# Softmax of the even heads: one ACTIVATE per head with an accumulated row sum, in place of subtract, one wide exponential and a reduction

## The chip, the cores and the metric

One core of a Trainium2 chip runs the whole program in one launch. The metric is device time in microseconds; the median of 3 runs is used. About 0.2% (9.5 us) is what a measurement of this kernel can tell from no change.

## The reference, cut to what matters

The input is `x` of shape (4, 512, 128). Four residual blocks follow each other: a gated linear attention, a transformer stack, a Mamba block, and the same transformer stack again. The change touches only the attention of the transformer stack, which runs twice with 6 layers each:

```python
def attn_layer(x, Wqkv, qs, ksc, Wo):        # HEADS 16, DIM_HEAD 64, WINDOW 32
    q, k, v = split(x @ Wqkv)                # per head
    q = l2norm(q) * qs; k = l2norm(k) * ksc
    q, k = rotary(q), rotary(k)
    # local attention: each window of 32 queries sees the 32 keys before it and its own 32
    sim = einsum('bhwie,bhwje->bhwij', bq, bk2) * QK_SCALE     # QK_SCALE 8
    sim = where(mask, -max, sim)
    attn = softmax(sim, -1)                  # over 64 keys
    out = einsum('bhwij,bhwje->bhwie', attn, bv2)
    return out @ Wo
for i in range(6):
    x = attn_layer(shift_tokens(x), ...) + x
    x = ffn_layer(shift_tokens(x), ...) + x  # layer norm, W1, a * gelu(gate), W2
```

So for every query and head there is a softmax over 64 scores: a maximum, an exponential of 8 * (score - max), and a sum by which the output is divided.

## The kernel before, in words

Each engine has its own hand-written instruction stream, tied to the others by counting semaphores; an engine works strictly in the order of its stream. The transformer stack is called a phase here: 24 bodies (6 layers x 4 batch rows), twice, so 48 bodies. A body handles one batch row of one layer and consists of 4 units (u = 0 to 3), one tile of 128 tokens each: 192 units in all. Most bodies run inside a hardware loop (`Fori`) on every engine, so there is a jump back once per body.

The work is software-pipelined. In unit u of a body, `pe_body`, `act_body`, `dve_body` and the loop in `pool_ffn` work on several tiles at once:
- the projection of tile u+2 in chunks of 512 columns (`pe_proj`, three matmuls per chunk, L273 to L275, chunk 0 one unit earlier than the rest). Chunks 0 to 3 are queries and keys: ScalarE squares each (`act_square`, L512), VectorE multiplies each by the rotary tables (`dve_rotate`, L693 to L695) and sums the squares (L696). VectorE waits at L691 for the square of the same chunk. Chunks 4 and 5 are values, copied out by ScalarE (`act_v`, L520);
- the norms of tile u+2 (`dve_rnorm` L716 to L723 on VectorE, `pool_newton` on GpSimd), and the rotated rows on GpSimd (L907, L913);
- the transposes of queries and keys of tile u+1 (`pe_qk_t`, L301), copied out by ScalarE (`act_qk_t`, L541), its scores (`pe_scores`, L329, L336) and its softmax (`dve_softmax_in`, `act_exp_odd`, `act_exp_even`);
- the transposed probabilities (`pe_probs_t`, L317, copied by `act_probs_t`, L548), the product with the values (`pe_pv`, L350) and the division (`dve_den`, `dve_out`, L760) of tile u;
- the output transposes of tile u-1 (L287, L530), and pieces of the projection Wo (L373) and of the MLP of the body before (L407, L408, L416; `act_gelu` L590, `act_std` L578, `dve_wo` L767, `dve_hidden` L796, `dve_down` L803).

The 16 heads are 8 pairs. Even heads (par 0, g = 0) have their scores in PSUM bank `s_ps[0]`, odd heads (g = 1) in `s_ps[1]`; each bank is 128 rows x 8 heads x 64 scores.

The softmax before: for the odd heads VectorE takes the maximum (L734) and scales it by -8 (L738, `bias_done`); ScalarE does 8 exponentials, one per head, each with that head's bias and an accumulated row sum (L558; the trace shows each as an ACTIVATE and an ACTIVATION_READ_ACCUMULATOR). For the even heads VectorE takes the maximum (L734) and subtracts it from the scores of all 8 heads in one instruction (L743, `sub_done`), ScalarE does one exponential over all 512 columns (L565, `exp0_done`), and VectorE reduces it to the row sums at the start of the next unit (L749 in `dve_den`), before the reciprocal (L753).

The order of ScalarE's stream around the change, from the end of one unit to the next:

```python
act_probs_t(it, u)            # L548
act_v(it, u + 2, 0); act_v(it, u + 2, 1)
act_exp_odd(it, u + 1)        # 8 x L558
act_square(it, u + 3, 0)      # L512
act_exp_even(it, u + 1)       # L565
# next unit (u is one higher now)
act_qk_t(it, u + 1, (0, 1))   # L541 q_t
act_square(it, u + 2, 1)      # L512
act_qk_t(it, u + 1, (2, 3))   # L541 k_t
```

VectorE's order in a unit is: rotate chunks 0 and 1, `dve_den`, `dve_xs`, rotate chunks 2 and 3, `dve_rnorm`, the pieces of the MLP, `dve_softmax_in`, `dve_out`. The queue of SyncE issues 16 DMAs per unit that copy the values into window pairs (`sp_pairs`, L943); `act_v` of the next tile waits for their landing.

## Time and profile before

| what | value |
|---|---|
| median of 3 runs | 4733.21 us (4729.46 to 4737.49) |
| span of the profiled execution | 4761.0 us |
| VectorE (DVE) busy | 3952.0 us, 83% |
| TensorE (PE) busy | 3888.7 us, 82% |
| ScalarE (ACT) busy | 2715.4 us, 57% |
| GpSimd (POOL) busy | 2320.0 us, 49% |
| mean granted TensorE clock | 0.906 |

For the profiled execution the span from its first to its last instruction is the only time that is given; it is 27.8 us (0.6%) above the median of the unprofiled runs. Busy shares are averages over the whole span; the transformer phases lie at about 120 to 2200 us and 2760 to 4640 us.

### The profile page before, as it was taken

To read this page: it belongs to the slowest core of one execution; us is meant where nothing else is said; L and a number is where in the kernel's file an instruction comes from. 1 tells how busy PE (TensorE), PEld (TensorE's weight loads), DVE (VectorE), ACT (ScalarE), POOL (GpSimd) and SP (SyncE) were. 2 spreads that over 40 slices of the span, in tenths; PEclk is the share of its full clock that TensorE was granted. 3 is DMA by queue.
4 is the path that set the end of the run, shared out by engine and by line. 5 is a ranking of instruction groups with operands and counts; after the bars stand their busy time and mean duration, and the time that the engine had idled before them with its cause. 6 is when DMAs were issued, how large, how long until landed. Compare 5 with 4: busy or idle time off the path is not lost. (4 is left out here: it accounts for less than half of the span.)

```text
span 4761.0 us, 167496 instructions
## 1 busy us (share of the span) xinstructions
PE 3888.7 (82%) x62204; PEld 2492.3 (52%) x62204; DVE 3952.0 (83%) x8550; ACT 2715.4 (57%) x6877; POOL 2320.0 (49%) x2468
## 2 busy tenths in 40 slices
PE   7788888888888888885655788888888888888887
PEld 2555565555555555552111365655655555555554
DVE  7798888888888888875888798888888888888884
ACT  2466566666656666662333366565656666566664
POOL 3455555555545555541444555455545545555551
PEclk9899999999989899996677789999998998998998
DMA  1222222222222222220000122222222222222221
GB/s 33 62 75 74 69 73 69 73 68 76 74 66 76 67 71 71 72 71 15 0 0 0 30 67 67 73 73 70 73 72 70 66 76 71 71 73 67 74 68 50
DMA packets 249055, 293.99 MB, mean 62 GB/s; under 512 B 61326, under 2 KB 136198, under 8 KB 248326
## 3 DMA queue, kind: packets, MB, share of 16 engines
q1 hardware_dynamic: 248446, 284.34, 23.2%
q8 instruction: 569, 9.32, 0.8%
q14 instruction: 40, 0.33, 0.0%
HBM read 81.75 MB, written 1.05 MB: 17 GB/s over the span
## 5 line engine op out<-in xcount | busy, mean ns | idle before, releaser
L907 POOL TENSOR_TENSOR qk_rows<-rot_cos,rot_sin 128x512 f32<-128x512 f32 x768 | 980.9, 1277 | 1468.0 <-DVE rot_sin L695 1463.9
L913 POOL TENSOR_TENSOR qk_rows<-qk_rows,rnorm 128x512 f32<-128x512 f32 x768 | 814.5, 1091 | 15.0
L273 PE MATMUL psum<-wqkv_hi,xs_hi 128*128 (+1 forms) x1152 | 627.2, 544 | 219.7 <-DVE x_ffn L803 60.6
L301 PE MATMUL psum<-ident,qk_rows 128*128 128x128 f32 x3072 | 550.1, 330 | 306.2 <-issue 152.5
L693 DVE TENSOR_TENSOR rot_cos<-psum,rot_scaled 128x512 f32<-128x512 f32 x768 | 528.3, 688 | 292.1 <-ACT squares L512 276.9
L520 ACT ACTIVATE v_rows<-psum 128x512 f32<-128x512 f32 x384 | 223.8, 597 | 889.1 <-PE psum L275 702.0
L301 PEld LDWEIGHTS psum<-ident,qk_rows 128*128 128x128 f32 x3072 | 434.0, 170 | 466.5 <-issue 320.3
L512 ACT ACTIVATE squares<-psum 128x512 f32<-128x512 f32 x768 | 479.0, 624 | 246.6 <-PE psum L275 238.5
L696 DVE TENSOR_REDUCE sumsq<-squares 128x8 f32<-128x512 f32 x768 | 518.5, 675 | 0.0
L558 ACT ACTIVATE probs<-psum,row_max_scaled 128x64 f32<-128x64 f32 x1536 | 457.4, 324 | 77.3 <-DVE row_max_scaled L738 75.4
L274 PE MATMUL psum<-wqkv_lo,xs_hi 128*128 (+1 forms) x1152 | 488.1, 424 | 0.0
L275 PE MATMUL psum<-wqkv_hi,xs_lo 128*128 (+1 forms) x1152 | 484.7, 421 | 0.0
L273 PEld LDWEIGHTS psum<-wqkv_hi,xs_hi 128*128 128x128 f32 x1152 | 237.7, 206 | 342.5 <-issue 309.8
L1408 POOL TENSOR_TENSOR mb_hc<-mb_h,mb_c 128x512 f32<-128x512 f32 x128 | 211.3, 1670 | 348.3 <-DVE mb_h L1377 331.3
L350 PE MATMUL psum<-v_pairs,probs_t 64*32 64x64 f32 x24576 | 354.0, 229 | 32.8 <-issue 28.8
L350 PEld LDWEIGHTS psum<-v_pairs,probs_t 64*32 64x32 f32 x24576 | 278.3, 108 | 178.4 <-issue 177.8
L373 PE MATMUL psum<-o_t,wo 128*128 128x512 f32 x768 | 351.9, 601 | 9.1 <-issue 8.4
L336 PEld LDWEIGHTS psum<-k_t,q_t 64*32 64x32 f32 x24576 | 269.3, 105 | 149.9 <-issue 149.6
L558 ACT ACTIVATION_READ_ACCUMULATOR probs<-psum,row_max_scaled 128x1 f32 x1536 | 332.9, 217 | 0.0
L336 PE MATMUL psum<-k_t,q_t 64*32 64x64 f32 x24576 | 331.7, 224 | 1.5 <-issue 1.4
L695 DVE TENSOR_TENSOR rot_sin<-psum,rot_scaled 128x256 f32<-128x256 f32 x768 | 318.0, 414 | 0.0
L694 DVE TENSOR_TENSOR rot_sin<-psum,rot_scaled 128x256 f32<-128x256 f32 x768 | 318.0, 414 | 0.0
(165 smaller groups left out, 7536.2 us busy)
## 6 DMA issues: line engine op xcount, KB each, us to landing
v_pairs<-v_rows SPq DMA_DIRECT2D x3072, 64.0 KB, 2.0
wo<-in_Wo SPq DMA_DIRECT2D x48, 512.0 KB, 4.3
wqkv_staged<-in_Wqkv SPq DMA_DIRECT2D x52, 384.0 KB, 3.2
w<-in_W SPq DMA_DIRECT2D x48, 341.0 KB, 3.1
qk_scale<-in_qk_scale SPq DMA_DIRECT2D x48, 128.0 KB, 3.1
w<-in_W SPq DMA_DIRECT2D x48, 128.0 KB
w<-in_W SPq DMA_DIRECT2D x48, 42.5 KB
rot_base<-in_rot SPq DMA_DIRECT2D x2, 512.0 KB, 3.4
```

The costliest lines, as they stand in the source:

```text
L273: nc.tensor.matmul(proj_ps[c % 2], xh, wh, start=True, stop=False)
L274: nc.tensor.matmul(proj_ps[c % 2], xh, wl, start=False, stop=False)
L275: nc.tensor.matmul(proj_ps[c % 2], xl, wh, start=False, stop=True).then_inc(S["qkv_mm"], 1)
L301: last = nc.tensor.transpose(tr_ps[g % 2][:, i * P:(i + 1) * P], m["qk"][:, u % 2, (4 * g + i) * P:(4 * g + i + 1) * P], ident[:, :])
L336: last = nc.tensor.matmul(s_ps[par][WIN * w:WIN * w + WIN, 64 * hp:64 * hp + 64], m["qt"][rows, hp, WIN * w:WIN * w + WIN], m["kt"][rows, ...
L350: last = nc.tensor.matmul(o_ps[par][WIN * w:WIN * w + WIN, 64 * hp:64 * hp + 64], m["pt"][rows, hp, WIN * w:WIN * w + WIN], m["vp"][rows, ...
L512: nc.scalar.activation(m["sq"][:, c % 2, :], proj_ps[c % 2], ACT.Square).then_inc(S["sq_done"], 1)
L558: last = nc.scalar.activation(m["p"][:, hp, 1, :], s_ps[1][:, 2 * WIN * hp:2 * WIN * (hp + 1)], ACT.Exp, scale=QK_SCALE, bias=m["nmax"][:, ...
L693: V.tensor_tensor(ma, ps, cos, ALU.mult)
L696: V.tensor_reduce(m["ss"][:, HC * c:HC * c + HC], m["sq"][:, c % 2, :].rearrange("p (h e) -> p h e", e=DH), AX.X, ALU.add)\
L907: G.tensor_tensor(qk[:, c * CH:(c + 1) * CH], m["ma"][:, c % 2, :], m["mb"][:, c % 2, :], ALU.add)\
L913: G.tensor_tensor(part, part, m["rn"][:, u % 2, HC * c:HC * c + HC].unsqueeze(2) .to_broadcast([P, HC, DH]), ALU.mult).then_inc(S["rot_don ...
```

## The change

The even heads are treated as the odd ones. `row_max_scaled` gets a column block for each parity; VectorE writes the scaled maximum of both (L738); the subtraction (L743) and the reduction (L749) go away. ScalarE does 8 exponentials per head straight from `s_ps[0]`, with bias and accumulated sum, at the place in its stream where the wide exponential was. The bank `s_ps[0]` is released to the next scores by `exp0_done` instead of `sub_done`.

```diff
-            m["nmax"] = fsb("row_max_scaled", [P, HP])
+            m["nmax"] = fsb("row_max_scaled", [P, 2, HP])
...
-                    wait(nc.tensor, S["exp1_done" if g else "sub_done"], cnt(it, 1, u))
+                    wait(nc.tensor, S["exp1_done" if g else "exp0_done"], cnt(it, 1, u))
...
-        def act_exp_odd(it, u):
-            nc.scalar.wait_ge(S["bias_done"], cnt(it, 1, u, 1))
+        def act_exp(it, u, g):
+            nc.scalar.wait_ge(S["bias_done"], cnt(it, 2, u, 2 - g))
             wait(nc.scalar, S["pT_mm"], cnt(it, 2, u))
             wait(nc.scalar, S["den_done"], cnt(it, 1, u))
             for hp in range(HP):
-                last = nc.scalar.activation(m["p"][:, hp, 1, :], s_ps[1][:, 2 * WIN * hp:2 * WIN * (hp + 1)], ACT.Exp,
-                                            scale=QK_SCALE, bias=m["nmax"][:, hp:hp + 1],
-                                            accum_out=m["den"][:, 1, hp:hp + 1])
-            last.then_inc(S["exp1_done"], 1)
-
-        def act_exp_even(it, u):
-            nc.scalar.wait_ge(S["sub_done"], cnt(it, 1, u, 1))
-            nc.scalar.activation(m["p"][:, :, 0, :], m["p"][:, :, 0, :], ACT.Exp, scale=QK_SCALE)\
-                .then_inc(S["exp0_done"], 1)
+                last = nc.scalar.activation(m["p"][:, hp, g, :], s_ps[g][:, 2 * WIN * hp:2 * WIN * (hp + 1)], ACT.Exp,
+                                            scale=QK_SCALE, bias=m["nmax"][:, g, hp:hp + 1],
+                                            accum_out=m["den"][:, g, hp:hp + 1])
+            last.then_inc(S["exp1_done" if g else "exp0_done"], 1)
...
                 if nxt:
-                    act_exp_odd(it, u + 1)
+                    act_exp(it, u + 1, 1)
                 if ahead or u + 3 < TILES:
                     act_square(it, u + 3, 0)
                 if nxt:
-                    act_exp_even(it, u + 1)
+                    act_exp(it, u + 1, 0)
...
-                if g == 1:
-                    wait(V, S["exp1_done"], cnt(it, 1, u))
-                    V.tensor_scalar(m["nmax"][:, :], m["mx"][:, 1, :], -QK_SCALE, None, ALU.mult)\
-                        .then_inc(S["bias_done"], 1)
-                else:
-                    wait(V, S["pT_mm"], cnt(it, 2, u))
-                    wait(V, S["den_sum"], cnt(it, 1, u))
-                    V.tensor_tensor(m["p"][:, :, 0, :], s, m["mx"][:, 0, :].unsqueeze(2).to_broadcast([P, HP, 2 * WIN]),
-                                    ALU.subtract).then_inc(S["sub_done"], 1)
+                wait(V, S["exp1_done" if g else "exp0_done"], cnt(it, 1, u))
+                V.tensor_scalar(m["nmax"][:, g, :], m["mx"][:, g, :], -QK_SCALE, None, ALU.mult)\
+                    .then_inc(S["bias_done"], 1)
 
         def dve_den(it, u):
             V.wait_ge(S["exp0_done"], cnt(it, 1, u, 1))
-            wait(V, S["den_done"], cnt(it, 1, u))
-            V.tensor_reduce(m["den"][:, 0, :], m["p"][:, :, 0, :], AX.X, ALU.add).then_inc(S["den_sum"], 1)
-            V.wait_ge(S["den_sum"], cnt(it, 1, u, 1))
             V.wait_ge(S["exp1_done"], cnt(it, 1, u, 1))
```

## Rows read from the trace of the kernel before

**Rows 1.** The page, its head and part 1: span, busy time of each engine.

```profile
span 4761.0 us, 167496 instructions
...
PE 3888.7 (82%) x62204; PEld 2492.3 (52%) x62204; DVE 3952.0 (83%) x8550; ACT 2715.4 (57%) x6877; POOL 2320.0 (49%) x2468
```

**Rows 2.** Waits by total over the span: engine line <- releaser: us, times, longest.

```profile
DVE rot_cos L693 <- ACT squares L512: 276.9, 222, 4.6
...
ACT v_rows L520 <- DMA v_pairs<-v_rows: 187.1, 60, 6.7
...
DVE x_ffn L767 <- PE psum L373: 40.1, 30, 10.8
```

**Rows 3.** Groups by line and shape: count | busy us, mean ns of one | idle before.

```profile
L558 ACT ACTIVATE probs<-psum,row_max_scaled 128x64 f32<-128x64 f32 x1536 | 457.4, 324 | 77.3 <-DVE row_max_scaled L738 75.4
...
L558 ACT ACTIVATION_READ_ACCUMULATOR probs<-psum,row_max_scaled 128x1 f32 x1536 | 332.9, 217 | 0.0
...
L743 DVE TENSOR_TENSOR probs<-psum,row_max 128x512 f32<-128x512 f32 x192 | 132.8, 692 | 13.4 <-DVE row_max L734 8.2
...
L749 DVE TENSOR_REDUCE den<-probs 128x8 f32<-128x512 f32 x192 | 129.9, 676 | 0.0
```

**Rows 4.** Timeline of ScalarE, units 2 and 3: start us, us, instruction, [idle <-releaser].

```profile
1048.32 0.31 ACT L558 ACTIVATE probs<-psum,row_max_scaled 128x64 f32<-128x64 f32 x1
...
1050.64 0.63 ACT L512 ACTIVATE squares<-psum 128x512 f32<-128x512 f32 x1
1051.12 0.68 ACT L565 ACTIVATE probs<-probs 128x512 f32<-128x512 f32 x1
1051.64 1.13 ACT L541 ACTIVATE q_t<-psum 128x512 f32<-128x512 f32 x2
1052.60 0.66 ACT L512 ACTIVATE squares<-psum 128x512 f32<-128x512 f32 x1
```

**Rows 5.** Timeline of VectorE over the same stretch.

```profile
1048.66 0.69 DVE L743 TENSOR_TENSOR probs<-psum,row_max 128x512 f32<-128x512 f32 x1
1049.27 1.28 DVE L760 TENSOR_TENSOR o_rows<-psum,rden 128x512 f32<-128x512 f32 x2
1051.31 0.69 DVE L693 TENSOR_TENSOR rot_cos<-psum,rot_scaled 128x512 f32<-128x512 f32 x1 [0.76 <-ACT squares L512]
...
1053.29 0.69 DVE L693 TENSOR_TENSOR rot_cos<-psum,rot_scaled 128x512 f32<-128x512 f32 x1
...
1055.96 0.67 DVE L749 TENSOR_REDUCE den<-probs 128x8 f32<-128x512 f32 x1
1056.67 0.25 DVE L753 RECIPROCAL rden<-den 128x16 f32<-128x16 f32 x1
```

**Rows 6.** Timeline of TensorE and of ScalarE at the jump back to the next body.

```profile
1074.57 1.96 PE L301 MATMUL psum<-ident,qk_rows 128*128 128x128 f32 x8 [4.06 <-issue]
...
1075.72 0.60 ACT L541 ACTIVATE q_t<-psum 128x512 f32<-128x512 f32 x1 [2.32 <-PE psum L301]
```

**Rows 7.** Timeline of ScalarE and VectorE in unit 1, before its exponentials.

```profile
1027.71 1.08 ACT L520 ACTIVATE v_rows<-psum 128x512 f32<-128x512 f32 x2 [3.48 <-DMA v_pairs<-v_rows]
...
1030.11 0.31 ACT L558 ACTIVATE probs<-psum,row_max_scaled 128x64 f32<-128x64 f32 x1
...
1028.94 0.17 DVE L738 TENSOR_SCALAR row_max_scaled<-row_max 128x8 f32<-128x8 f32 x1
```

**Rows 8.** Timeline of VectorE: second rotation at the start of unit 2.

```profile
1035.46 0.69 DVE L693 TENSOR_TENSOR rot_cos<-psum,rot_scaled 128x512 f32<-128x512 f32 x1 [0.42 <-ACT squares L512]
```

**Rows 9.** Timeline of VectorE and ScalarE late in unit 3, around the gate.

```profile
1060.74 0.75 DVE L796 SCALAR_TENSOR_TENSOR hidden<-psum,layer_vectors,gelu 85x512 f32<-85x512 f32 x1 [0.72 <-ACT gelu L590]
...
1059.54 0.60 ACT L512 ACTIVATE squares<-psum 128x512 f32<-128x512 f32 x1 [1.84 <-PE psum L275]
```

**Rows 10.** Timeline of ScalarE and VectorE at the start of unit 1: second square and rotation.

```profile
1016.95 0.66 ACT L512 ACTIVATE squares<-psum 128x512 f32<-128x512 f32 x1
...
1017.64 0.69 DVE L693 TENSOR_TENSOR rot_cos<-psum,rot_scaled 128x512 f32<-128x512 f32 x1
```

More of the change, by code:

```diff
@@ L249, in build @@
             "seed", "newton", "add_done", "rot_done", "v_ev", "vp0", "vp1", "oT_mm", "oT_ev", "qkT_mm",
-            "qkT_ev", "s_mm", "max_done", "bias_done", "sub_done", "den_sum", "exp1_done", "exp0_done", "den_done", "pT_mm", "pT_ev",
+            "qkT_ev", "s_mm", "max_done", "bias_done", "exp1_done", "exp0_done", "den_done", "pT_mm", "pT_ev",
             "o_mm", "o_ev", "wo_in", "w1_in", "w2_in", "vec_in", "qks_in", "rots_done", "d1_mm", "d1_ev",
@@ L637, in act_ffn @@
             act_qk_t(first, 0, range(4))
-            act_exp_odd(first, 0)
+            act_exp(first, 0, 1)
             act_square(first, 2, 0)
-            act_exp_even(first, 0)
+            act_exp(first, 0, 0)
             act_body(first, False, True)
```

## The prediction

> **What bounds the kernel now.** I read the page first. VectorE is busy 83% of the span, TensorE 82%, ScalarE 57% [rows 1], which invites the reading that VectorE is the bound and ScalarE has room. So I looked next at who waits for whom: VectorE's largest wait of the transformer phases is the rotation L693 for ScalarE's squares, 276.9 us in 222 waits [rows 2]. ScalarE, the less busy engine, already holds up the busier one. The third view, the timelines of one body, says where. ScalarE starts 8 odd exponentials at 1048.32, the first square at 1050.64, the even exponential at 1051.12, the two q_t copies at 1051.64, the second square at 1052.60 [rows 4]. VectorE waits 0.76 us for the first square and starts the rotation of chunk 1 at 1053.29, 0.03 us after the second square ends (1052.60 + 0.66) [rows 4, 5]. At the start of every unit, then, the time is handed along ScalarE's queue: bias, odd exponentials, square, even exponential, q_t, square, and only then VectorE goes on. What is put in at the place of the even exponential moves VectorE's second rotation unless something else was late there.
>
> **The change, part by part.**
>
> ScalarE, added: one head costs (1050.64 - 1048.32) / 8 = 0.29 us from start to start [rows 4]. Its two records are 324 and 217 ns [rows 3] and overlap. Eight even heads therefore take 2.32 us, and the one wide exponential that goes took 1051.64 - 1051.12 = 0.52 us [rows 4]: +1.80 us in each of 192 units, 346 us of ScalarE's time. The page ScalarE: Activation LUTs of the Trainium skill (section What ACT_TABLE_LOAD costs) says that an ACTIVATE with a pointer bias takes about 280 ns and 0.833 ns per column, and that neighbours overlap by about 93 ns. By that page alone, as an estimate, 8 heads of 64 columns take 1.92 us and the addition is 1.40 us; the trace's 0.29 us per head holds the accumulator read too, and it decides. No table load is added: the square between the exponentials is followed by the next one 0.48 us later, with none between [rows 4].
>
> VectorE, removed: the subtraction, 1049.27 - 1048.66 = 0.61 us from start to start, and the reduction, 1056.67 - 1055.96 = 0.71 us [rows 5] (busy 692 and 676 ns [rows 3]). Added: a second scaling of a maximum, 0.17 us [rows 7]. That is 1.15 us less per unit, 221 us of VectorE's time. The subtraction lies between the odd bias, which has already been sent off, and the output division; after that VectorE waits 0.76 us for the first square [rows 5], whose time is set by the odd exponentials. So its 0.44 us net only lengthens that wait: I count it at nothing (if the wait were absent it would be worth 0.44 us). The reduction comes after the second rotation, and its 0.71 us does count wherever VectorE is the one that is late afterwards.
>
> Waits and storage: TensorE's next scores of the even bank now wait for the end of the exponentials instead of the subtraction. In TensorE's stream these scores stand behind the probabilities' transposes, which need both exponentials now and needed them before; nothing is added. No DMA and no queue of SyncE or GpSimd changes; behind the longer exponentials on ScalarE stand q_t, the square of chunk 1, k_t, the gelu and o_t, and for these TensorE and VectorE wait.
>
> Now the four places per body.
>
> - Start of unit 1 (the even exponential of the tile issued in unit 0). The second rotation started at 1017.64, 0.03 us after its square ended (1016.95 + 0.66) [rows 10]: +1.80. The missing reduction takes 0.71 back: VectorE is 1.1 us late for the rest of unit 1. There ScalarE waits 3.48 us for a DMA before its v copies, then copies, loads its table and starts the exponentials at 1030.11, while the bias was written by 1029.11 [rows 7]. The 1.1 us falls into this 1.0 us: 0.1 is left. These waits for the DMA are 187.1 us in 60 times over 48 bodies [rows 2], so it is there in most bodies.
> - Start of unit 2. VectorE had waited 0.42 us for the second square [rows 8], and TensorE's projection, not only ScalarE's queue, was late by a little: I count 1.45 of the 1.80. With 0.1 carried in and 0.71 taken back, 0.85 is left, and it goes through maximum, bias and table load to the next exponentials, because there is no DMA wait in this unit.
> - Start of unit 3. +1.80 in full (margin 0.03 us above). It now stands at 2.65. The reduction gives nothing back here: later in the unit VectorE already waits 0.72 us for the last gelu, which stands behind the fourth square, for which ScalarE waits 1.84 us on TensorE [rows 9], and TensorE's stream has passed the k_t copy, 1.8 us later. What VectorE saves, it waits at the gate.
> - Start of unit 0 (the jump to the next body). TensorE stands still 4.06 us at the jump and ScalarE idles 2.32 us before q_t [rows 6]. The 1.80 fits in; nothing is added. This is the cover on which the place rests; without the stall at the jump it would cost up to 1.80 more. The reduction here could give 0.71 back, but VectorE then meets TensorE at the x_ffn addition, where it waited 40.1 us in 30 of 48 bodies [rows 2]: I take 0.2.
>
> Sum per body: 0.1 + 0.75 + 1.8 - 0.2 = 2.45 us. I take 46 of the 48 bodies, since the last of each phase has no tiles ahead: +113 us. Against the profiled span that is 4761 to 4874. The median of the runs is 27.8 us below that span, and I carry the difference over unchanged: 4733 + 113 = **4846 us**, 2.4% slower. I assume that TensorE's granted clock stays as it is.
>
> Bounds of this case. Low: the reduction counts everywhere outside unit 1, 1.1 + 0.75 + 0.1 - 0.7 = 1.25 per body, +57 us. High: the DMA wait swallows only half, +0.9 more per body, and 0.2 is not given back, 3.55 per body, +163 us.
>
> **The rivals.**
>
> A, VectorE is the bound (faster). The mechanism is VectorE's own stream: if its work per unit, not the square, sets the time of the next unit, all 1.15 us per unit come off, 4733 - 221 = 4512 us. For it: the 83% busy, the highest of all engines [rows 1]. Against: the 276.9 us of waits for squares, and the 0.03 us margin at the second one. It decides from the point where ScalarE's slack before the second square is over 1.80 us; I saw that only at the jump. The Trainium skill's page Perfetto Trace Analysis, section Identifying the Most-Contended Engine, says to optimize the engine of highest occupancy first; by that rule the change takes work from the right engine and is this rival.
>
> B, ScalarE's addition goes through nearly whole (slower still). If neither the DMA wait nor the reduction takes anything back, three places count: 1.8 + 1.45 + 1.8 = 5.05 per body, times 46, +232, 4965 us. For it: k_t, gelu and o_t are all behind in the same queue, and TensorE's stream follows them. Against: the DMA wait in unit 1.
>
> C, it cancels. The slack in other bodies is larger than in the one I walked, some 1.5 us at each of the three places, and the reduction's 0.71 counts: within 9.5 us of 4733. For it: waits for squares come in 222 pieces of different length up to 4.6 us. Against: the places recur with small margins.
>
> D, the change doesn't do what it says: if the 8 small exponentials of the second bank overlapped down to the 0.217 us of their read record [rows 3], ScalarE would get 8 x 0.217 - 0.52 = 1.22 us more a unit, and the places 0, 0.16, 1.22 and -0.2: 1.2 per body, +55 us, 4788. Nothing in the odd heads' rows speaks for that.
>
> **How the numbers follow.** Forecast 0.66, A with partial forms of it 0.12, B 0.08, C 0.07, D 0.07. Slower by over 0.2% (9.5 us, about what a measurement of this kernel tells from no change): 0.66 + 0.08 + 0.07 = 0.81. Same 0.07, faster 0.12. The range begins at C's middle, rounded to 4740, and leaves A and about half of C below; above it goes beyond the +163 and part of the way to B, 4925.
>
> **What would show it.** Right: 3072 records of L558's successor with the same 0.29 us pitch, none of the subtraction and reduction; ScalarE busy up by about 300 us; VectorE busy down some 200 but idle up by more; the wait of the rotation L693 for squares more than doubled, above all before chunk 1, in units 1 to 3; the span up by 2.4 us a body. The step of unit 1 is right if its exponentials start as soon after the DMA's landing as before. Wrong: VectorE's busy share rises, or the wait for squares stays near 277 us; or the loss sits at the jump.

## The result, and the profile after

The changed kernel takes **5137.1 us** (median of 4 runs, 5127.05 to 5145.59) beside 4731.3 us of the kernel before on the same chip (4728.56 to 4737.49): ratio 1.0849 (95% interval 1.0831 to 1.0867), 406 us slower. Forecast were 4846 us and a range of 4740 to 4925. The direction was right. The size was not: the loss is more than three times the forecast's 113 us, and above rival B's 4965 us too.

The head of the page of the changed kernel, with the busy times, answers to [rows 1]:

```profile
span 5133.2 us, 170227 instructions
...
PE 4013.3 (78%) x62204; PEld 2549.7 (50%) x62204; DVE 3889.6 (76%) x8358; ACT 3085.0 (60%) x9757; POOL 2316.7 (45%) x2468
```

ScalarE has 369.6 us more work (3085.0 - 2715.4), within 7% of the 346 us that the prediction counts. VectorE has only 62.4 us less (3952.0 - 3889.6), where I had counted 221. TensorE does the same 62204 matmuls and shows 124.6 us more busy time, while the mean granted clock went from 0.906 to 0.879.

The changed kernel's waits (engine, line, what released it: us in total, times, longest); the first and the `v_rows` line answer to [rows 2]:

```profile
DVE rot_cos L688 <- ACT squares L512: 424.6, 281, 2.4
...
PE psum L301 <- ACT q_t L541: 344.0, 159, 5.5
...
DVE hidden L782 <- ACT gelu L585: 185.2, 56, 4.7
...
DVE rot_cos L688 <- issue: 99.8, 27, 5.1
ACT L558 <- DVE row_max_scaled L732: 97.7, 93, 2.7
...
ACT v_rows L520 <- DMA v_pairs<-v_rows: 61.7, 31, 4.3
```

The same view of the kernel before has these for TensorE's wait for q_t and VectorE's for the gelu:

```profile
DVE hidden L796 <- ACT gelu L590: 72.0, 56, 4.7
...
PE psum L301 <- ACT q_t L541: 31.9, 45, 3.0
```

VectorE's wait for the squares rose by half and did not more than double. But the total hides two opposite moves. Laid on the intervals described below, two thirds of the 277 us before lie in the interval with the jump and some 90 us in the other three; in the changed kernel it is 80 and 344. Where the prediction expected the loss, the wait nearly quadrupled; the large wait that it had started from lay mostly at the jump. What grew most is TensorE's wait for q_t, tenfold. And there is a wait that the kernel before does not have at all: 97.7 us in which ScalarE stands before an instruction of L558 with no tile in its name. The groups by line and shape (count | busy us, mean ns of one | idle before and what ended it) say which instruction that is:

```profile
L558 ACT ACTIVATE probs<-psum,row_max_scaled 128x64 f32<-128x64 f32 x3072 | 927.2, 357 | 76.3 <-DVE row_max_scaled L732 74.6
L558 ACT ACTIVATION_READ_ACCUMULATOR probs<-psum,row_max_scaled 128x1 f32 x3072 | 766.2, 250 | 0.0
...
L732 DVE TENSOR_SCALAR row_max_scaled<-row_max 128x8 f32<-128x8 f32 x384 | 197.5, 514 | 13.3
L558 ACT ACT_TABLE_LOAD x138 | 177.1, 1283 | 98.5 <-DVE row_max_scaled L732 97.7
...
L659 DVE TENSOR_SCALAR xs_hi<-x_ffn 64x128 fp32r x344 | 118.5, 344 | 5.4
```

It is the table load. The same three groups of the kernel before:

```profile
L558 ACT ACT_TABLE_LOAD x138 | 177.1, 1283 | 2.4
...
L664 DVE TENSOR_SCALAR xs_hi<-x_ffn 64x128 fp32r x344 | 76.4, 222 | 17.5
...
L738 DVE TENSOR_SCALAR row_max_scaled<-row_max 128x8 f32<-128x8 f32 x192 | 69.4, 362 | 6.6
```

No load was added (138 in both), but its wait went from 2.4 to 98.5 us. And a scaling of a maximum, which I had costed at 0.17 us, takes 0.51 us on average; before it took 0.36.

**Where in a body.** I took the start of the first maximum of each tile as a mark (L734 before, L729 after) and measured from mark to mark, averaged over the 22 middle bodies of each of the two phases. In the kernel before the marks of the body of [rows 4 to 10] are these; the last interval of a body holds the jump. The last line is one of its scalings, for step 2 of the account below:

```profile
1011.66 0.69 DVE L734 TENSOR_REDUCE row_max<-psum 128x8 f32<-128x512 f32 x1
...
1028.23 0.68 DVE L734 TENSOR_REDUCE row_max<-psum 128x8 f32<-128x512 f32 x1
...
1047.15 0.68 DVE L734 TENSOR_REDUCE row_max<-psum 128x8 f32<-128x512 f32 x1
...
1067.31 0.68 DVE L734 TENSOR_REDUCE row_max<-psum 128x8 f32<-128x512 f32 x1
...
1068.03 0.95 DVE L738 TENSOR_SCALAR row_max_scaled<-row_max 128x8 f32<-128x8 f32 x1
```

| interval (what it holds) | before, us | forecast | measured | e1 |
|---|---|---|---|---|
| first (second rotation of unit 1) | 16.56 | +1.1 | +1.76 | +1.69 |
| second (DMA wait, start of unit 2) | 19.07 | -0.25 | +1.73 | +0.27 |
| third (start of unit 3, the gate) | 20.17 | +1.8 | +5.08 | +2.98 |
| fourth (the jump) | 27.48 | -0.2 | -0.70 | -0.41 |
| a body | 83.28 | +2.45 | +7.87 | +4.53 |

The forecast column is the prediction's own four places laid on these intervals (1.0 us of the first place was to be absorbed by the DMA wait in the second interval: -1.0 + 1.45 - 0.71 is about -0.25). 48 bodies by 7.87 are 378 us; the two profiled spans differ by 372. The profiled execution before was 27.8 us above its median and the one after 4 us below, so the medians show some 30 us more than the profiles do. A single entry of the table carries the scatter of one profiled execution. e1 is the first experiment. The table says that the first place lost 0.7 us more than forecast, the second 2.0 and the third 3.3, and that the jump hid the addition, as forecast.

### The profile page after: what moved, and what is told of

Its sections match the earlier page's. It is cut to its first block and busy times, and to the rows that moved or that the text cites. A ratio compares the mean times of both kernels' runs of the same rounds, so it can differ in the third digit from the quotient of the medians.

```text
span 5133.2 us, 170227 instructions
## 1 busy us (share of the span) xinstructions
PE 4013.3 (78%) x62204; PEld 2549.7 (50%) x62204; DVE 3889.6 (76%) x8358; ACT 3085.0 (60%) x9757; POOL 2316.7 (45%) x2468
## 5 line engine op out<-in xcount | busy, mean ns | idle before, releaser
L893 POOL TENSOR_TENSOR qk_rows<-rot_cos,rot_sin 128x512 f32<-128x512 f32 x768 | 977.4, 1273 | 1834.4 <-DVE rot_sin L690 1834.3
L301 PE MATMUL psum<-ident,qk_rows 128*128 128x128 f32 x3072 | 529.0, 322 | 592.0 <-ACT q_t L541 344.0
L558 ACT ACTIVATE probs<-psum,row_max_scaled 128x64 f32<-128x64 f32 x3072 | 927.2, 357 | 76.3 <-DVE row_max_scaled L732 74.6
L688 DVE TENSOR_TENSOR rot_cos<-psum,rot_scaled 128x512 f32<-128x512 f32 x768 | 529.0, 689 | 532.5 <-ACT squares L512 424.6
L301 PEld LDWEIGHTS psum<-ident,qk_rows 128*128 128x128 f32 x3072 | 404.9, 164 | 776.7 <-issue 704.7
L273 PE MATMUL psum<-wqkv_hi,xs_hi 128*128 (+1 forms) x1152 | 651.4, 565 | 150.9 <-DVE x_ffn L789 60.1
L558 ACT ACTIVATION_READ_ACCUMULATOR probs<-psum,row_max_scaled 128x1 f32 x3072 | 766.2, 250 | 0.0
L512 ACT ACTIVATE squares<-psum 128x512 f32<-128x512 f32 x768 | 491.0, 639 | 316.2 <-PE psum L275 308.6
L275 PE MATMUL psum<-wqkv_hi,xs_lo 128*128 (+1 forms) x1152 | 498.2, 432 | 0.0
L274 PE MATMUL psum<-wqkv_lo,xs_hi 128*128 (+1 forms) x1152 | 498.0, 432 | 0.0
```

Of the source, the lines that this page charges most:

```text
L273: nc.tensor.matmul(proj_ps[c % 2], xh, wh, start=True, stop=False)
L274: nc.tensor.matmul(proj_ps[c % 2], xh, wl, start=False, stop=False)
L275: nc.tensor.matmul(proj_ps[c % 2], xl, wh, start=False, stop=True).then_inc(S["qkv_mm"], 1)
L301: last = nc.tensor.transpose(tr_ps[g % 2][:, i * P:(i + 1) * P], m["qk"][:, u % 2, (4 * g + i) * P:(4 * g + i + 1) * P], ident[:, :])
L512: nc.scalar.activation(m["sq"][:, c % 2, :], proj_ps[c % 2], ACT.Square).then_inc(S["sq_done"], 1)
L558: last = nc.scalar.activation(m["p"][:, hp, g, :], s_ps[g][:, 2 * WIN * hp:2 * WIN * (hp + 1)], ACT.Exp, scale=QK_SCALE, bias=m["nmax"][:, ...
```

## The experiments

Each ran beside runs of the kernel before, whose median was 4733.6 us for e1 to e4, 4737.6 us for e5 to e8 and 4742.0 us for e9 to e11 (4731.3 us beside the changed kernel). The ratios are those on record; they lie up to 0.16% from the quotients of these medians. So a difference between experiments of different groups is uncertain by some 10 us beyond the scatter of the runs.

### e1: the wait for the bias put last

```diff
         def act_exp(it, u, g):
-            nc.scalar.wait_ge(S["bias_done"], cnt(it, 2, u, 2 - g))
-            wait(nc.scalar, S["pT_mm"], cnt(it, 2, u))
             wait(nc.scalar, S["den_done"], cnt(it, 1, u))
+            wait(nc.scalar, S["pT_mm"], cnt(it, 2, u))
+            nc.scalar.wait_ge(S["bias_done"], cnt(it, 2, u, 2 - g))
```

> The changed kernel with the three waits ahead of each set of exponentials in another order: the wait for the scaled maximum last, so that inside the loop it belongs to the first exponential and the table load runs before it, as in the kernel before. Theory 'table load behind the wait': the changed kernel shows 97.7 us of idle time before table loads (93 times) that the kernel before did not have; these go, 5137 becomes about 5040, and unit 1 takes about 1 us less from maximum to maximum. Rival 'only ScalarE's longer work counts': within 15 us of 5137.

Measured: 5001.5 us, ratio 1.0568 (1.0540 to 1.0596). Three waits in another order in the source take 136 us off the changed kernel, more than the 97 us expected. In the changed kernel ScalarE's timeline in unit 1 and VectorE's over the same stretch are (start us, us, instruction, [idle before]):

```profile
1020.81 1.09 ACT L520 ACTIVATE v_rows<-psum 128x512 f32<-128x512 f32 x2 [2.43 <-DMA v_pairs<-v_rows]
...
1023.13 0.17 DVE L732 TENSOR_SCALAR row_max_scaled<-row_max 128x8 f32<-128x8 f32 x1
...
1023.40 1.28 ACT L558 ACT_TABLE_LOAD   x1 [1.51 <-DVE row_max_scaled L732]
...
1024.70 0.31 ACT L558 ACTIVATE probs<-psum,row_max_scaled 128x64 f32<-128x64 f32 x1
```

The v copies end at 1021.90, and the table could load then. ScalarE stands until the bias is written (1023.13 + 0.17) and loads afterwards: 1.51 us idle, then 1.28 us for the load. In e1 the load follows the copies, and the groups give its wait as 14.7 us in all (the lines are from a unit 1 whose copies waited for TensorE and not for the DMA):

```profile
1084.77 0.60 ACT L520 ACTIVATE v_rows<-psum 128x512 f32<-128x512 f32 x1 [1.15 <-PE psum L275]
1085.39 1.28 ACT L558 ACT_TABLE_LOAD   x1
1086.68 0.31 ACT L558 ACTIVATE probs<-psum,row_max_scaled 128x64 f32<-128x64 f32 x1
```

So it is in the kernel before too: the table loads while the bias is written at 1028.94, and the exponentials start at 1030.11 [rows 7]:

```profile
1028.81 1.28 ACT L558 ACT_TABLE_LOAD   x1
```

The source has the three waits in the same order before and after the change. What differs is where they end up in ScalarE's compiled stream of a loop body. This is an extract of the programs, not a view of the profile (before, changed, e1):

```text
L554 REGISTER_ALU
L558 ACT_TABLE_LOAD [waits den_done,pT_mm]
L558 ACTIVATE probs,den<-psum,row_max_scaled 128x64 [waits bias_done]

L554 REGISTER_ALU
L71 REGISTER_ALU [waits pT_mm,bias_done]
L558 ACT_TABLE_LOAD
L558 ACTIVATE probs,den<-psum,row_max_scaled 128x64 [waits den_done]

L71 REGISTER_ALU
L556 REGISTER_ALU [waits pT_mm,den_done]
L558 ACT_TABLE_LOAD
L558 ACTIVATE probs,den<-psum,row_max_scaled 128x64 [waits bias_done]
```

In the kernel before, the first ACTIVATE carries the wait for the bias, and the load ahead of it does not. The change counts the bias twice a unit, its count needs a register calculation of its own, and the wait for it is now carried by such a calculation, ahead of the load. In e1 the wait that comes last in time is behind the load again. The traces agree: in the changed kernel a register instruction that waits for the bias stands at 1023.34, between the bias (1023.30) and the load (1023.40). By the table e1 wins 1.5 us in the second interval and 2.1 us in the third; the third is taken up under e9.

### e3: only ScalarE's addition

Applied to the kernel before. Subtraction and reduction stay, the wide exponential becomes 8 with an accumulated sum (which the reduction overwrites, so the row sums are the old ones).

```diff
-            nc.scalar.activation(m["p"][:, :, 0, :], m["p"][:, :, 0, :], ACT.Exp, scale=QK_SCALE)\
-                .then_inc(S["exp0_done"], 1)
+            for hp in range(HP):
+                last = nc.scalar.activation(m["p"][:, hp, 0, :], m["p"][:, hp, 0, :], ACT.Exp,
+                                            scale=QK_SCALE, bias=eps_t[:, :],
+                                            accum_out=m["den"][:, 0, hp:hp + 1])
+            last.then_inc(S["exp0_done"], 1)
```

> The kernel before with the even exponential split into 8 per head with bias and accumulated sum, in place; subtraction and reduction on VectorE stay, the table load stays early. Theory 'the removed VectorE work is worth next to nothing': same as the run with reordered waits within 40 us, so some 300 us over the kernel before. Rival 'VectorE's savings count': slower than the run with reordered waits by more than 100 us, up to 221.

Measured: 5041.1 us, ratio 1.0656 (1.0625 to 1.0687), +307 us; 40 us above e1, at the edge of what was expected. Here a head is read from SBUF and takes 0.33 us from start to start, so the addition is 8 x 0.33 - 0.52 = 2.13 us a unit. By the marks: +2.10, +1.32, +2.18, +0.14. The first and third intervals get it whole, the second gets it less 0.8, the jump hides it. A cover of 0.8 us in the second interval exists, then. The prediction had two there, 1.0 us of the DMA wait and 0.35 us before the square of unit 2; their sum is too large by half a microsecond, and e3 does not tell the two apart. VectorE's rows show the handing-on, a wait of 1.89 us before the second rotation, where the kernel before had 0.42 [rows 8]:

```profile
1106.53 0.69 DVE L696 TENSOR_TENSOR rot_cos<-psum,rot_scaled 128x512 f32<-128x512 f32 x1 [1.89 <-ACT squares L512]
1109.52 0.75 DVE L790 SCALAR_TENSOR_TENSOR xn_mlp<-ln_xc,layer_vectors,psum 128x512 f32<-128x512 f32 x1 [1.04 <-PE psum L395]
```

Behind it VectorE waits again, 1.04 us for TensorE's L395, and TensorE had waited 0.72 us for q_t shortly before: what ScalarE adds reaches VectorE on a second way. At the changed kernel's 1.80 us a unit, e3's loss scales to 307 x 1.80 / 2.13 = 259 us (an estimate). That is the largest part of the 406. It is not ScalarE's queue alone: the two matmuls of L395 took 878 ns each on average in e3 and 747 ns in the kernel before, so some of it is TensorE's clock.

### e4: only VectorE's savings

e1 with the even heads' 8 exponentials replaced by a single wide one. It leaves out the even heads' row sums, with ones in their place, and takes head 0's maximum as the bias of all even heads.

```diff
+            if g == 0:
+                nc.scalar.activation(m["p"][:, :, 0, :], s_ps[0].rearrange("p (h k) -> p h k", k=2 * WIN), ACT.Exp,
+                                     scale=QK_SCALE, bias=m["nmax"][:, 0, 0:1]).then_inc(S["exp0_done"], 1)
+                return
             for hp in range(HP):
...
+            V.memset(m["den"][:, 0, :], 1.0)
```

> The changed kernel with one wide exponential for the even heads, straight from PSUM, with one head's bias for all of them; the even row sums are not computed (ones stand there) and the other heads' maxima are not applied. VectorE's savings without ScalarE's addition. Theory 'VectorE waits anyway': within 50 us of the kernel before, 4680 to 4740. Rival 'VectorE bound': 4510 to 4600.

Measured: 4687.5 us, ratio 0.9908 (0.9881 to 0.9936), -46 us. The page of e4:

```profile
PE 3835.0 (82%) x62204; PEld 2448.3 (52%) x62204; DVE 3875.9 (83%) x8360; ACT 2723.6 (58%) x6877; POOL 2324.6 (50%) x2468
```

VectorE is busy 76 us less than before, not 221, although both wide instructions are gone. So with no cost on ScalarE the change would be worth 46 us. By the marks they come from the second interval (-1.17 us) and the jump (-0.65); the first is 0.28 shorter and the third 0.39 longer. Where the rest of the saving went is seen in the changed kernel, on VectorE and GpSimd together:

```profile
1023.88 2.04 POOL L899 TENSOR_TENSOR qk_rows<-qk_rows,rnorm 128x512 f32<-128x512 f32 x2
...
1023.93 1.02 DVE L732 TENSOR_SCALAR row_max_scaled<-row_max 128x8 f32<-128x8 f32 x1
...
1025.06 1.41 DVE L765 SCALAR_TENSOR_TENSOR gelu<-ident,ln_col_rstd 128x512 f32<-128x512 f32 x1
```

The odd scaling at 1023.13 took 0.17 us, with GpSimd between two small instructions. The even one starts 0.05 us after a GpSimd instruction (of 1.04 us; the line holds two) and ends at 1024.95, 0.03 us after that one does. The multiplication at L765 takes 1.41 us where L779 took 0.73 us. And where the reduction stood there is now `xs_hi`; in units 0 and 1 it begins while GpSimd's L893 runs (at 1013.96 in unit 1, L893 from 1013.37 to 1014.66) and two take 1.04 instead of 0.47 us, in units 2 and 3 of this body 0.41. Its mean is 344 instead of 222 ns. Busy time adds up: 132.8 + 129.9 us removed [rows 3]; put back are 197.5 - 69.4 = 128.1 for the scalings, 118.5 - 76.4 = 42.1 for this form of `xs_hi`, and about 48 x (1.377 - 0.729) = 31.1 for L765. That leaves 61.4 us; the page says 62.4. Smaller groups that I left out change by up to 7 us each, and records overlap, so that the two agree within 1 us is chance.

The Trainium skill, page SBUF — State Buffer, section SBUF: two separate sides, says that VectorE and GpSimd share a pair of ports as an exclusive lock held for a whole instruction, which concerns VectorE's instructions in a two-port mode or with two inputs in SBUF. The trace agrees for the scaling, which ends 0.03 us after the GpSimd instruction that ran when it began; the other two are longer where GpSimd works beside them. The prediction did not weigh it.

### e6 and e7: the maximum written negated

If the scaling is gone, its price is seen. q_t is multiplied by 8 in its copy, and the maximum's reduction writes its negative. e6 is e1 with this; e7 is the kernel before with this for its odd heads.

```diff
...
-                V.tensor_reduce(m["mx"][:, g, :], s, AX.X, ALU.max).then_inc(S["max_done"], 1)
-                V.wait_ge(S["max_done"], cnt(it, 2, u, n + 1))
                 wait(V, S["exp1_done" if g else "exp0_done"], cnt(it, 1, u))
-                V.tensor_scalar(m["nmax"][:, g, :], m["mx"][:, g, :], -QK_SCALE, None, ALU.mult)\
-                    .then_inc(S["bias_done"], 1)
+                V.tensor_reduce(m["nmax"][:, g, :], s, AX.X, ALU.max, negate=True).then_inc(S["bias_done"], 1)
```

> As the run with reordered waits, but the reduction writes the negated maximum and the q_t copy carries the factor 8, so that no scaling instruction of 128x8 remains on VectorE (two per unit go, 0.37 and 0.66 us on the mean; the second ends 25 ns after the GpSimd instruction that ran when it began). Theory 'VectorE's saving was eaten by these': VectorE busy falls by about 196 us, the bias is there 0.5 to 0.7 us sooner where VectorE sets it, and the time falls by 40 to 100 us against the run with reordered waits. Rival 'ScalarE's queue alone': within 20 us of it.

> The kernel before with the same replacement for the odd heads alone (the even heads keep subtraction, wide exponential and reduction). One instruction of 0.36 us mean goes from ahead of the odd exponentials in each of 192 units, 69 us. Theory 'what stands between scores and square is on the path': 20 to 70 us under the kernel before, and by that the fastest so far. Rival 'no effect': within 10 us.

Measured: e6 4935.4 us, ratio 1.0409 (1.0392 to 1.0427), 66 us below e1 (75 us by the ratios). VectorE's busy time:

```profile
PE 3910.9 (79%) x62204; PEld 2488.2 (50%) x62204; DVE 3658.7 (74%) x7974; ACT 3066.8 (62%) x9757; POOL 2321.0 (47%) x2468
```

That is 216.6 us less work on VectorE than in e1 (3875.3), for 66 us of time: about a third of the work removed counts. VectorE's wait for the squares rises from 344.5 to 440.2 us, so much of the rest is waited away. e7: 4719.3 us, ratio 0.9961 (0.9940 to 0.9981), 18 us faster than the kernel before, just under the 20 us expected at least. It is the fastest kernel of this study that computes everything.

### e2: the even exponentials behind the second square

If the loss comes from VectorE waiting for the square, moving the exponentials behind it should give it back. e2 is e1 with this.

```diff
                     act_square(it, u + 2, 1)
+                act_exp(it, u, 0)
...
-                if nxt:
-                    act_exp(it, u + 1, 0)
```

`u` is one higher at the new place, so it is the same tile.

> As the run with reordered waits, and the 8 even exponentials moved on ScalarE behind the q_t copies and the square of chunk 1. Theory 'the loss is handed on by ScalarE's queue to q_t and the square, and by the late q_t to TensorE's clock': both are out of the way, and the time falls by more than 150 us against the run with reordered waits, to 4850 or less. Rival 'ScalarE's work counts wherever it stands' (k_t, o_t and the gelu stand behind it too): within 60 us of the run with reordered waits.

Measured: 4965.9 us, ratio 1.0495 (1.0467 to 1.0523), only 36 us below e1: the rival's case. VectorE's wait for the squares falls from e1's 344.5 us to 168.0, and others take its place:

```profile
PE psum L287 <- ACT k_t L541: 341.2, 187, 3.7
DVE hidden L780 <- ACT gelu L585: 257.7, 100, 4.8
...
DVE rot_cos L686 <- ACT squares L512: 168.0, 190, 3.7
```

k_t and the gelu stand in the same queue, and now they are late. At the one other place that was tried the addition costs nearly as much. The square was the first to wait for it, not the only one.

### e5, e9 and e11: TensorE's clock in unit 3

The third interval grew by 5.08 us, where e3, with the larger addition, has 2.18. TensorE's clock is one difference between the two. The stretches of the changed kernel around TensorE's wait for q_t in unit 3 (window: us, busy us of each engine, granted clock, DMA share, GB/s):

```profile
1047.00:1052.00 5.00, 3.20 (x15) 1.69 (x12) 3.02 (x6) 5.00 (x31) 3.26 (x3) 1.00 0.28 69
1052.00:1055.60 3.60, 2.25 (x11) 1.45 (x12) 2.53 (x5) 3.57 (x7) 1.15 (x1) 0.68 0.43 109
1055.60:1061.00 5.40, 5.38 (x15) 3.32 (x16) 3.15 (x10) 2.04 (x4) 1.38 (x2) 0.58 0.25 62
1061.00:1066.00 5.00, 5.00 (x84) 3.27 (x83) 3.33 (x6) 2.73 (x5) 1.26 (x1) 1.00 0.01 3
```

and TensorE's timeline in them:

```profile
1052.15 1.12 PE L301 MATMUL psum<-ident,qk_rows 128*128 128x128 f32 x8 [1.95 <-ACT q_t L541]
1055.62 1.94 PE L287 MATMUL psum<-ident,o_rows 128*128 128x128 f32 x8 [1.22 <-ACT k_t L541]
1057.35 1.92 PE L407 MATMUL psum<-xn_mlp,w 128*85 128x512 f32 x2
1059.06 1.57 PE L408 MATMUL psum<-xn_mlp,w 128*85 128x512 f32 x2
```

TensorE stands 1.95 us for q_t up to 1052.15, with the clock at its upper level (granted 1.00, 2.4 GHz). In the 3.60 us from 1052.00 the mean is 0.68: the clock falls there to the lower level (0.5, 1.2 GHz), before the wait of 1.22 us for k_t: the matmul of L274 at 1053.35 takes 0.63 us, the one at 1047.85 took 0.40. Most of the 5.4 us from 1055.60 also run at the lower level (mean 0.58), then it is 1.00 again. Two matmuls of L407 take 1.92 us; the kernel before has there:

```profile
1056.84 1.02 PE L407 MATMUL psum<-xn_mlp,w 128*85 128x512 f32 x2
1057.70 1.02 PE L408 MATMUL psum<-xn_mlp,w 128*85 128x512 f32 x2
```

What follows, the square for the gate, is late: VectorE waits 3.77 us for the last gelu in this body, before 0.72 [rows 9]. To test it, five additional matmuls, whose result nothing reads, stand in TensorE's wait for q_t. They write the bank of the odd scores and so wait for the odd exponentials. e5 has them in every unit of the changed kernel, e9 only in unit 3, e11 is e1 with them in unit 3.

```diff
                 if nxt:
+                    if u == 3:                # e9, e11; e5 without the two conditions on u
+                        nc.tensor.wait_ge(S["exp1_done"], cnt(it, 1, u, 1))
+                    for _ in range(5 if u == 3 else 0):
+                        nc.tensor.matmul(s_ps[1], onehot[64:128, 0, :], maskrow[64:128, :], start=True, stop=True,
+                                         skip_group_check=True)
                     pe_qk_t(it, u + 1, prev, (2, 3))
```

> The changed kernel with 5 matmuls of 64x512 bf16 in TensorE's stream ahead of the transposes of k in each unit, about 1.9 us of work whose result nothing reads, where TensorE waits some 2 us for the late q_t copy. Theory 'part of the loss is TensorE's granted clock, which falls after that wait': the mean clock rises from 0.879 to 0.90 or more, the third interval from maximum to maximum falls from 25.4 us by more than 1 us, and the time falls by 40 to 120 us. Rival 'the clock is a side effect, the stream is bound elsewhere': the time stays within 15 us of 5137 or rises.

> The changed kernel with the 5 filler matmuls in unit 3 alone. With them in all units the interval of unit 3 fell from 25.25 to 23.10 us, and the one that holds the jump rose from 26.78 to 29.19. Theory 'the clock costs about 2 us in unit 3, and the filler cost it back at the jump': unit 3 again 23.1, the jump's interval back near 26.8, so 5137 falls by 80 to 110 us. Rival 'what the filler gains in unit 3 is only moved to the jump': the time stays within 20 us of 5137.

> The run with reordered waits plus the filler matmuls in unit 3 alone. Theory 'part of the 136 us that the reordering gave was the clock': the filler brings less here than on the changed kernel, 20 to 60 us under 5001, and what is left over the kernel before is 1.80 us in three units of a body, 46 x 5.4 = 248 us, less what VectorE gives back: 4940 to 4980. Rival 'the two are independent': 80 to 110 us under 5001.

Measured: e5 5149.5 us, ratio 1.0868 (1.0848 to 1.0888), no gain, though the mean clock rises from 0.879 to 0.901. By the marks it wins 2.2 us in the third interval (23.10 against 25.25) and loses 2.4 at the jump (29.19 against 26.78), by the additional matmuls there or by the wait ahead of them. e9, without them at the jump: 5081.9 us, ratio 1.0733 (1.0712 to 1.0754), 55 us below the changed kernel and less than the 80 to 110 expected, with a third interval of 23.32 and 27.48 at the jump. The groups of the slowed matmuls, first of the changed kernel, then of e9 (where they are at L408):

```profile
L407 PE MATMUL psum<-xn_mlp,w 128*85 128x512 f32 x96 | 78.8, 917 | 4.5 <-DVE hidden L782 4.5
```

```profile
L408 PE MATMUL psum<-xn_mlp,w 128*85 128x512 f32 x96 | 49.3, 595 | 4.5 <-DVE hidden L788 4.5
```

The matmuls are back at the 595 ns of the kernel before. So the fallen clock of unit 3 costs the changed kernel some 55 us at the least. In the second interval the clock is lower too (the matmuls of L395 take 1017 ns instead of 747, and still 984 in e9); what that costs no run shows. e11: 5022.1 us, ratio 1.0608 (1.0587 to 1.0629), outside both expectations: no gain over e1 but 21 us more, which the intervals of the two ratios do not quite keep apart. With the table load early the matmuls of L407 already take only 644 ns in e1, so there is little left to win (its third interval goes from 23.15 to 22.83 us), while the second interval and the jump grow by 0.3 and 0.8 us. The four kernels make a square: with the additional matmuls the order of waits is worth 5081.9 - 5022.1 = 60 us, without them 136. If the additional matmuls cost the same at other places in both, the difference of 76 us, with some 20 us of uncertainty, is what the late table load costs by way of the clock in unit 3. The third intervals alone say the same: 48 x (1.93 - 0.32) = 77 us.

### e8 and e10: the other direction, and the one place that hides it

e8 treats the odd heads as the even ones are treated in the kernel before: subtract, a wide exponential, and one reduction for both.

```diff
-            for hp in range(HP):
-                last = nc.scalar.activation(m["p"][:, hp, 1, :], s_ps[1][:, 2 * WIN * hp:2 * WIN * (hp + 1)], ACT.Exp,
...
+            nc.scalar.activation(m["p"][:, :, 1, :], m["p"][:, :, 1, :], ACT.Exp, scale=QK_SCALE)\
+                .then_inc(S["exp1_done"], 1)
...
+                V.tensor_tensor(m["p"][:, :, g, :], s, m["mx"][:, g, :].unsqueeze(2).to_broadcast([P, HP, 2 * WIN]),
+                                ALU.subtract).then_inc(S["sub_done"], 1)
```

> The change turned round: both parities with subtraction on VectorE and one wide exponential, and one reduction over both. ScalarE gets 1.8 us less per unit, VectorE about 1.2 us more. Theory 'the path runs through ScalarE': ScalarE's 1.8 in three units a body outweighs VectorE's, 4640 to 4740. Rival 'VectorE is close behind as a bound': 4780 to 4900.

Measured: 4750.9 us, ratio 1.0026 (1.0015 to 1.0038), 13 us slower, between what the theory and the rival expected. The page:

```profile
PE 3856.0 (81%) x62204; PEld 2467.1 (52%) x62204; DVE 4100.2 (86%) x8550; ACT 2410.0 (51%) x3997; POOL 2320.5 (49%) x2468
```

305 us are taken from ScalarE and 148 given to VectorE for next to no change. One parity each way is a balance. In the kernel before, 76 us less on VectorE are worth 46 (e4), 305 less on ScalarE do not pay for 148 more on VectorE, and more on ScalarE costs three quarters of its length: 307 of 192 x 2.13 = 409 us (e3). Less work on ScalarE alone was not tried.

e10 is e7 with the change for tile 0 of each body alone. Its even exponentials are issued in unit 3 and meet the stall at the jump, the one interval in which nothing was lost.

```diff
+            if u % TILES == 0:
+                for hp in range(HP):
+                    last = nc.scalar.activation(m["p"][:, hp, 0, :], s_ps[0][:, 2 * WIN * hp:2 * WIN * (hp + 1)],
+                                                ACT.Exp, scale=1.0, bias=m["nmax"][:, 0, hp:hp + 1],
+                                                accum_out=m["den"][:, 0, hp:hp + 1])
+                last.then_inc(S["exp0_done"], 1)
+                return
...
```

> The kernel before with negated maxima, and the change made for tile 0 of each body alone, whose even exponentials fall into TensorE's stall at the jump; tiles 1 to 3 keep subtraction, wide exponential and reduction. Theory 'the addition is hidden at the jump, and only there VectorE's saving is left over': the interval that holds the jump falls by 0.3 to 0.7 us a body against the run with negated maxima on the kernel before (4719), 15 to 35 us, to 4684 to 4704. Rival 'the stall hides VectorE's saving as well': within 8 us of 4719.

Measured: 4726.9 us (12 runs), ratio 0.9976 (0.9963 to 0.9989): faster than the kernel before, not faster than e7 (0.9961, intervals overlap). The jump's interval is 26.55 us against e7's 26.86, so the addition is hidden there. The 0.3 us of saving that the marks suggest (15 us in 48 bodies) does not show in the run time.

## Why the prediction was right or wrong

**Right.** The pitch of 0.29 us a head: in the changed kernel the 8 even exponentials go from 1027.51 to the q_t copy at 1029.82, 2.31 us, forecast 2.32. The way of the loss, handed along ScalarE's queue to the second rotation: it waits 1.89 us in units 1, 2 and 3 of the body read. The stall at the jump as a cover: the fourth interval did not grow (-0.70, forecast -0.2). Rival A was rightly rejected, but partly by luck: e4, with no price on ScalarE, gains 46 us and not 221, yet VectorE's work fell by only 76 us there. Of what was really saved more than half counted. The reason given, that VectorE only waits longer, explains the smaller part; the larger is that most of the saving never was one. A cover in the second interval exists as well, but e3 shows 0.8 us of it, where the DMA wait and the slack in unit 2 were counted at 1.35.

**Wrong, by steps.**

1. "No table load is added." True, and beside the point: I counted loads and not what stood ahead of them. The doubled count of the bias put its wait ahead of the load, and the load went from beside the bias to behind it. This costs 136 us (e1), of which 60 are left with the additional matmuls in place and some 76 go by way of the clock in unit 3. This is the largest single miss. It undid the cover in the second interval: +1.73, where e1 has +0.27.

2. "Added: a second scaling of a maximum, 0.17 us." The row is like three of the four in the body read. The fourth, at 1068.03, began 0.11 us into a GpSimd instruction and took 0.95 us; the four average 0.37 us, close to the group's 362 ns. The prediction's groups by line list the removed instructions [rows 3] and not that of the scaling. And a second scaling, 0.8 us behind the first, mostly falls into GpSimd's next long instruction. The second scaling costs 128.1 / 192 = 0.67 us, and two other VectorE instructions moved onto GpSimd's. The 221 us are 62.

3. "The missing reduction takes 0.71 back." The first interval grew by 1.76, not 1.1, and e1's by 1.69. `xs_hi` stands where the reduction stood and takes 1.04 instead of 0.47 us in unit 1, which eats 0.57 of the 0.71. In the second interval the reduction's 0.71 and the 1.45 come to +0.27 in e1, forecast -0.25.

4. "I assume that TensorE's granted clock stays as it is." It fell from 0.906 to 0.879. In unit 3 the cause is the late q_t, for which TensorE stands: matmuls in that wait bring the speed back. The third interval took +5.08 instead of +1.8; in e9 +3.15. This is worth at least 55 us (e9), which are largely in the 136 of the first step too. The 1.35 us by which e9 still exceeds the forecast are not explained by a run.

5. Rival B's price was computed for 5.05 us a body with no saving. ScalarE's part alone is some 259 us by e3, near to B's 232. So B was the better case for that term, and I gave it 0.08.

The sum: 259 (e3, scaled) - 46 (e4) + 136 (e1) = 349 of the 406 us. The 57 left have no run of their own, and their cause stays open. They are in e1 already, +268 where 259 - 46 would give 213, and by the marks over half of them lie in the third interval: +2.98 in e1, where e3, scaled, and e4 together give 2.2. That VectorE's saving is waited away once ScalarE's queue is late would fit a part; TensorE's lower clock in the second interval is another candidate.

**Open.** VectorE waits at the jump for nothing that the profile shows (`rot_cos L688 <- issue`, 99.8 us; 4.7 before, 34.5 in e4, 121.8 in e1). It costs nothing visible, as the fourth interval shrank. In the jump's interval this wait and the one for the squares make some 180 us together, where the kernel before has about as much for the squares alone, so it may be the same stall, put down to something else. The pages show one more thing that changed, the DMA queue that brings instructions, before and after:

```profile
q14 instruction: 40, 0.33, 0.0%
```

```profile
q14 instruction: 247, 2.02, 0.1%
```

The packets follow this wait through most runs: 36 to 40 where it is 5 us or less, 139 and 140 where it is 35 (e4, e10), 247 or more where it is 100 to 146. e3 is the exception, with 148 packets and 5.3 us. No run was made to test whether instructions that arrive late are the cause.

## What to carry to other kernels

Before adding an instruction to an engine with a low busy share, find which engine waits for which; ScalarE at 57% was the one that VectorE at 83% waited for, and what was added to it cost its whole length in two of four units and over half of it in a third (e3). Where a wait or its count changes ahead of a ScalarE function, look in the compiled stream where the table load stands: the wait that ends last in time should be behind it, on the ACTIVATE. Before taking work off an engine, split its largest wait by place; most of the 277 us that I started from lay at the jump, where nothing could be lost. Cost a small VectorE instruction between SBUF tensors by the mean of its group and by what GpSimd does at that time, not by its best row.

## What the runs showed of the hardware

- A 128x8 scaling on VectorE takes 0.17 us or, where that is later, lasts until 0.03 us after the end of the GpSimd instruction that runs when it begins: 1.02 us for the one at 1023.93. Writing the maximum negated in the reduction itself, which reads PSUM, removes it: 66 us in e6, 18 us in e7.
- A table load of 1.28 us runs beside the wait for its ACTIVATE's operand or only after it, by whether that wait stands behind the load or ahead of it: 12.4 us (e1) or 97.7 us of idle time before loads, and 136 us of run time.
- Five additional matmuls in a wait of about 2 us kept the clock up in unit 3: the 128x85 matmuls behind it took 595 instead of 917 ns (e9). At the jump the same five cost more than they gave (e5).
- An exponential of 64 columns and the read of its accumulated sum overlap, from one head to the next too: 0.29 us from head to head out of PSUM, 0.33 us out of SBUF (e3), with records of 357 and 250 ns in the changed kernel.
